# Computing the keys and values of a token tile in eight half-width groups instead of four full-width ones

## What is computed

```python
xn = _layernorm(x, axis=-1)
# attention branch
q = xn @ Wq + bq
kv = (xn @ Wdown + bdown) @ Wup + bup          # 1024 -> 256 -> 2048
q = q.reshape(B, T, H, Dh); kv = kv.reshape(B, T, H, 2 * Dh)
k, v = jnp.split(kv, 2, axis=-1)
q = apply_rope(q); k = apply_rope(k)
att = softmax(einsum('bthd,btgd->bthg', q, k) / sqrt(64))   # 16 x 16 per token
attn = einsum('bthg,btgd->bthd', att, v).reshape(B, T, D) @ Wout + bout
# expert branch: top-1 of 8
probs = softmax(xn @ router_w.T + router_b)
ffn = y_all[top1] * max(probs)
out = x + attn + ffn
```

## Time and profile before

| | us |
|---|---|
| median of 2 runs | 2858.91 |
| the 2 runs | 2851.67, 2866.16 |
| the profiled execution, on the device | 2871.62 |
| span of its slowest core (core 1) | 2870.1 |
| spans of its 8 cores | 2836.2 to 2870.1 |

### The profile page before, as it was taken

One profiled execution on the slowest core, in us unless ns is written; L12 is line 12 of the kernel. 1 busy time (PEld: TensorE's weight loads), 2 busy tenths in 40 slices (PEclk: granted clock), 3 DMA queues, 4 the chain that ended last, 5 costly groups with the idle time before them and its releaser, 6 DMA issues.

```text
span 2870.1 us, 38972 instructions; the slowest of 8 cores (2836.2 to 2870.1 us)
## 1 busy us (share of the span) xinstructions
PE 1937.4 (68%) x16622; PEld 1561.4 (54%) x16622; DVE 859.9 (30%) x1041; ACT 558.5 (19%) x770; POOL 106.6 (4%) x210
## 2 busy tenths in 40 slices
PE   0112268687776868686868778686868687777867
PEld 0112247465665746564756556564647475665646
DVE  2111132332324242323333232423232332324241
ACT  0122231221212030312122121203031211212030
POOL 0000000000000000000000000000000000000000
PEclk9956569688887869696978778787969787887869
DMA  5465515142332414151524234251415152332413
GB/s 161 138 206 199 190 59 206 59 178 87 141 124 91 175 59 174 38 201 59 192 73 177 88 118 147 80 185 39 169 58 206 59 184 81 140 125 94 157 59 132
DMA packets 60798, 366.45 MB, mean 128 GB/s; under 512 B 7107, under 2 KB 8131, under 8 KB 26580
## 3 DMA queue, kind: packets, MB, share of 16 engines
q1 hardware_dynamic: 31828, 179.41, 18.8%
q0 software_dynamic: 28800, 184.56, 16.9%
HBM read 330.39 MB, written 33.55 MB: 127 GB/s over the span
## 4 chain that ended last, share of the span: by engine, by line
PE 58%; DMA 17%; DVE 9%; ACT 8%; issue 4%; DVEq 2%; ACTq 2%; SPq 1%; POOL 0%; POOLq 0%
PE psb L814 26%; DMA exbuf<-exscratch 10%; PE psb L764 7%; PE psb L729 5%; DMA y_f<-exw 5%; PE psb L866 4%; PE psa L721 4%; ACT koct L584 2%; ACT vdm L589 2%; PE psa L752 2%; PE psa L879 2%; DVE exbuf L299 1%; ACTq L509 1%; DVEq L216 1%; DVE pav L463 1%
## 5 line engine op out<-in xcount | busy, mean ns | idle before, releaser
L814 PE MATMUL psb<-xe,exbuf 128*128 128x256 bf16 x8192 | 971.4, 284 | 131.5 <-DVE xe L472 68.8
L814 PEld LDWEIGHTS psb<-xe,exbuf 128*128 128x128 bf16 x8192 | 827.6, 102 | 278.3 <-issue 155.9
L764 PE MATMUL psb<-lat,wup_sb 128*128 128x256 bf16 x1024 | 187.8, 361 | 122.9 <-ACTq L509 122.9
L472 DVE TENSOR_TENSOR xe<-xnf,mrep 128x2048 bf16<-128x2048 bf16 x96 | 116.2, 1224 | 471.1 <-PE psb L814 467.3
L764 PEld LDWEIGHTS psb<-lat,wup_sb 128*128 128x128 bf16 x1024 | 123.8, 125 | 187.3 <-issue 149.5
L695 PE MATMUL psa<-idbf,exbuf 128*128 128x128 bf16 x512 | 47.5, 270 | 203.5 <-DVE exbuf L299 198.3
L721 PE MATMUL psa<-rT_sb,xnf 128*128 128x8 f32 x512 | 111.5, 361 | 89.7 <-DVEq L216 89.7
L721 PEld LDWEIGHTS psa<-rT_sb,xnf 128*128 128x128 f32 x512 | 110.4, 332 | 93.2 <-issue 93.2
L695 PEld LDWEIGHTS psa<-idbf,exbuf 128*128 128x128 bf16 x512 | 43.3, 125 | 207.6 <-issue 207.5
L729 PE MATMUL psb<-xnf,wq_sb 128*128 128x256 bf16 x1024 | 154.1, 328 | 0.0
L729 PEld LDWEIGHTS psb<-xnf,wq_sb 128*128 128x128 bf16 x1024 | 122.1, 120 | 30.9
(11 more groups left out here) (123 smaller groups left out, 1620.7 us busy)
## 6 DMA issues: line engine op xcount, KB each, us to landing
exbuf<-exscratch SPq DMA_DIRECT2D x128, 1024.0 KB, 5.5
exbuf<-exscratch POOLq DMA_DIRECT2D x128, 1024.0 KB, 8.5
y_f<-exw SPq DMA_DIRECT2D x64, 512.0 KB
x_t<-x POOLq DMA_DIRECT2D x32, 512.0 KB, 5.1
exscratch<-exbuf POOLq DMA_DIRECT2D x8, 2048.0 KB, 10.6
out<-outsb POOLq DMA_DIRECT2D x32, 512.0 KB, 6.8
y_f<-wq SPq DMA_DIRECT2D x8, 512.0 KB
y_f<-wo SPq DMA_DIRECT2D x8, 512.0 KB
```

Source lines behind the costliest of these rows:

```text
L472: vector.tensor_tensor(out=re(xe[:, 2048 * (ex_i % 2):2048 * (ex_i % 2) + 2048], "p (cc t) -> p cc t", t=256), in0=src0, in1=m1.broadcast_ ...
L764: li = tensor.matmul(out=psb[:, 256 * gch:256 * (gch + 1)], lhsT=wup[:, 4096 * k + 128 * ch: 4096 * k + 128 * (ch + 1)], rhs=lat[:, 256 * ...
L814: li = tensor.matmul(out=pout(m), lhsT=exbuf[:, eb + 1024 * k + 128 * m: eb + 1024 * k + 128 * (m + 1)], rhs=xe[:, xb + 256 * k:xb + 256 * ...
```

## The change

The up-projection is cut into eight groups `kv0` to `kv7` of 8 matmuls (4 chunks) each, which write the lower and the upper half of `psb` (two banks each) in turn. TensorE waits before group r for the eviction of group r-2 and no longer for that of group r-1; the first two groups wait for `latev` and `qev`. ScalarE evicts each half with an instruction of 1024 elements per partition, with runs of 4 elements in the target instead of 8. The waits of VectorE and of the later `psb` user move from `kv1ev` to `kv3ev` and from `kv3ev` to `kv7ev`, which mark the same data.

```diff
 T_SLOTS = ['xnT', 'router', 'q', 'prepA', 'prepB', 'lat', 'kv0', 'kv1', 'kv2', 'kv3',
+           'kv4', 'kv5', 'kv6', 'kv7',
            'vT0', 'qk0', 'vT1', 'qk1', 'av0', 'av1', 'expert', 'wout', 'yT']
 S_SLOTS = ['apply', 'den', 'qev', 'latev', 'kv0ev', 'kv1ev', 'kv2ev', 'kv3ev',
+           'kv4ev', 'kv5ev', 'kv6ev', 'kv7ev',
            'vst0', 'extr0', 'vst1', 'exp0', 'extr1', 'exp1', 'of0', 'of1', 'nrinv']
...
@@ VectorE
                 vector.wait_ge(smS, sv(i, 'qev'))
-                vector.wait_ge(smS, sv(i, 'kv1ev'))
+                vector.wait_ge(smS, sv(i, 'kv3ev'))
...
-                vector.wait_ge(smS, sv(i, 'kv3ev'))
+                vector.wait_ge(smS, sv(i, 'kv7ev'))
...
@@ ScalarE
-                for r in range(4):
+                for r in range(8):
                     scalar.wait_ge(smT, tv(i, 'kv%d' % r))
                     if r == 0 and i > 0:
                         scalar.wait_ge(smT, tv(i - 1, 'qk1'))
-                    if r == 2 and i > 0:
+                    if r == 4 and i > 0:
                         scalar.wait_ge(smT, tv(i - 1, 'vT1'))
-                    if r < 2:
-                        srck = re(psb[:], "p (g og j) -> p og j g", og=32, j=8)
+                    hb = 1024 * (r % 2)
+                    if r < 4:
+                        srck = re(psb[:, hb:hb + 1024], "p (g og j) -> p og j g",
+                                  og=32, j=8)
                         dstk = re(koct[:], "p (og j gg) -> p og j gg", j=8,
-                                  gg=16)[:, :, :, 8 * r:8 * r + 8]
+                                  gg=16)[:, :, :, 4 * r:4 * r + 4]
                         scalar.copy(out=dstk, in_=srck)
                     else:
...
@@ TensorE
-                for r in range(4):
-                    tensor.wait_ge(smS, sv(i, 'latev'))
-                    tensor.wait_ge(smS, sv(i, 'qev') if r == 0 else sv(i, 'kv%dev' % (r - 1)))
-                    for gch in range(8):
-                        ch = 8 * r + gch
+                for r in range(8):
+                    if r == 0:
+                        tensor.wait_ge(smS, sv(i, 'latev'))
+                        tensor.wait_ge(smS, sv(i, 'qev'))
+                    elif r >= 2:
+                        tensor.wait_ge(smS, sv(i, 'kv%dev' % (r - 2)))
+                    hb = 1024 * (r % 2)
+                    for gch in range(4):
+                        ch = 4 * r + gch
                         for k in range(2):
-                            li = tensor.matmul(out=psb[:, 256 * gch:256 * (gch + 1)],
+                            li = tensor.matmul(out=psb[:, hb + 256 * gch:
+                                                       hb + 256 * (gch + 1)],
...
-                tensor.wait_ge(smS, sv(i, 'kv3ev'))
+                tensor.wait_ge(smS, sv(i, 'kv7ev'))
```

More of the change, by code:

```diff
@@ L577, in _ @@
                         scalar.wait_ge(smT, tv(i - 1, 'qk1'))
-                    if r == 2 and i > 0:
+                    if r == 4 and i > 0:
                         scalar.wait_ge(smT, tv(i - 1, 'vT1'))
-                    if r < 2:
-                        srck = re(psb[:], "p (g og j) -> p og j g", og=32, j=8)
+                    hb = 1024 * (r % 2)
+                    if r < 4:
+                        srck = re(psb[:, hb:hb + 1024], "p (g og j) -> p og j g",
+                                  og=32, j=8)
                         dstk = re(koct[:], "p (og j gg) -> p og j gg", j=8,
-                                  gg=16)[:, :, :, 8 * r:8 * r + 8]
+                                  gg=16)[:, :, :, 4 * r:4 * r + 4]
                         scalar.copy(out=dstk, in_=srck)
                     else:
-                        srcv = re(psb[0:64, :], "p (g og j) -> p og j g", og=32, j=8)
+                        srcv = re(psb[0:64, hb:hb + 1024], "p (g og j) -> p og j g",
+                                  og=32, j=8)
                         dstv = re(vdm[:], "p (og j gg) -> p og j gg", j=8,
-                                  gg=16)[:, :, :, 8 * (r - 2):8 * (r - 2) + 8]
+                                  gg=16)[:, :, :, 4 * (r - 4):4 * (r - 4) + 4]
                         scalar.copy(out=dstv, in_=srcv)
```

## The result

| | before | changed |
|---|---|---|
| median, us (10 and 11 runs) | 2868.65 | 2735.95 |
| ratio, 95% interval | | 0.9513 [0.9484, 0.9542] |
| profiled execution, us | 2871.62 | 2736.39 |
| spans of the cores, us | 2836.2 to 2870.1 | 2703.4 to 2734.8 |

The changed kernel is 4.9% faster: 0.0487 x 2868.65 = 140 us, where 115 us were forecast.

A forecast was written before the change was run, and what follows sets the result against it. The bound was taken to be TensorE and ScalarE in strict turns in the up-projection. 20.4 - 13.2 = 7.2 us per tile, times 16 = 115 us; 2858.9 - 115 = 2744 us (-4.0%), range 2705 to 2795 us.

The forecast's parts named there:

- What bounds the stage: Up-projection: TensorE matmuls and ScalarE evictions take strict turns with nothing beside them, 20.4 us a tile.
- Evictions: ScalarE's half evictions of 1024 elements in the up-projection: 1.05 us each, pitch 1.20 us with drain and signal.
- C: Rival: up-projection evictions cost by the run, a half takes 1.865 us; gain 50 us, 2809 us; chance 0.05.
- E: Rival: slower, short runs make a half eviction cost 2.435 us; +24 us, 2883 us; chance 0.03.
- I take the third: Clock case chosen for the up-projection: four groups low, then high; last eviction ends at 13.1 us.
- the 20.4 us before: Length per tile of the up-projection stage before the change, first matmul to VectorE's addition to the values (L407).
- The level of VectorE and ScalarE: End of the up-projection: VectorE free after q and k at 13.1 us, the same moment as `kv7ev`.
- No gain behind the stage: From `vT0` on the order is unchanged and the chain only moves up; no gain counted there.
- A: Rival: low clock for the whole up-projection stage, 15.1 us per tile; gain 85 us, 2774 us; chance 0.20.
- B: Rival: high clock throughout the up-projection stage, 10.9 us per tile; gain 152 us, 2707 us; chance 0.10.
- the forecast: Main case: up-projection stage falls from 20.4 to 13.2 us per tile; gain 115 us, 2744 us; chance 0.57.
- D: Rival: gain given back in the expert phase, TensorE's 62.3 us weight waits doubling; 2806 us; chance 0.05.

The follow-up runs named there:

- e9: e1 with six extra unused matmuls behind each half group, so turns stay but the clock is high; ratio to the kernel before 1.0008, stage 20.86 us.
- e4: Kernel before the change with 10 extra unused matmuls behind each of the four groups, filling TensorE's pauses; ratio to before 0.9846, stage 18.94 us.
- e1: Changed kernel with eight half groups, but TensorE waits for the eviction of the group just before (r-1), so no overlap; ratio to before 1.0256.
- e7: Changed kernel with 8 extra unused matmuls in TensorE's pause between the latent's matmuls and the up-projection; ratio to before 0.9478, stage 12.27 us.
- e2: Changed kernel with VectorE's addition to q moved ahead of its wait for kv3ev; ratio to before 0.9513.
- e3: Changed kernel with four half buffers in psb and psa instead of two, TensorE waiting for the eviction of group r-4; ratio to before 0.9530.
- e5: Changed kernel with q addition moved forward and four half buffers, ScalarE evicting keys and VectorE values with their bias; ratio to before 0.9300, stage 10.04 us.

## Why the prediction was right

**What bounds the stage.** TensorE and ScalarE in turns, with nothing beside them: right. e9 against the changed kernel shows 7.66 us per tile for the overlap, at a clock that was slightly higher in e9.

**Evictions.** 1.05 us were taken, 1.012 and 1.005 were measured; 1.20 us of pitch were taken, 1.16 measured. Rivals C and E needed 1.87 and 2.44 us and are out. No cost of the short runs is to be seen: 1012 ns with runs of 4 is not above the 1053 ns of the contiguous copy, and 2 x 1012 is 159 ns above 1865, which one fixed part per instruction would explain. The estimate from the Trainium skill ("ScalarE: Activation LUTs", What ACT_TABLE_LOAD costs), 1.04 us, is 3% above the trace; the page's figures are for ACTIVATE, and the instructions here are CAST.

**The clock: the step that was mis-sized.** "I take the third" stood for four groups, 32 matmuls, at the low clock. The traces have 14 to 19 in three tiles of four and none in the fourth, 12.3 on the mean. The fault was a misreading of rows 2. There the prediction says that the clock rose during `kv1`, "some 7 us on". Three stretches of that tile, `kv0` and the beginning and the end of `kv1` (length; busy us and instructions of PE, PEld, DVE, ACT, POOL; granted clock; DMA share; GB/s) say otherwise:

```profile
1171.15:1174.60 3.45, 3.45 (x16) 2.23 (x16) 0.00 (x0) 0.00 (x0) 0.00 (x0) 0.50 0.00 0
1176.90:1178.00 1.10, 1.10 (x11) 0.98 (x12) 0.00 (x0) 0.00 (x0) 0.00 (x0) 1.00 0.00 0
1178.10:1179.40 1.30, 1.29 (x7) 0.60 (x4) 0.00 (x0) 0.00 (x0) 0.00 (x0) 0.50 0.00 0
```

`kv0` ran at the low clock, and `kv1` began at the high one. Its 2.51 us are not a rise but a fall: the clock went back during it, after the pause of 2.2 us ahead of it. So 16 low matmuls came before the rise, not 32. A group of mixed speed does not tell which way the clock went. It is the rule and not this tile: of the 91 tiles of the kernel before whose stage begins at the low clock, 82 have the first 16 matmuls low and the 17th high. So the changed kernel does not raise its clock any sooner; it holds on to it, since the pauses are short.

With two groups low instead of four the prediction's own prices give 1.68 + 1.89 + 0.14 = 3.7 us for the start of the second eviction, 3.7 + 7 x 1.20 = 12.1 us for the end of the last, and 12.2 us for L409. The pitch of 1.16 us takes off 0.3 more. The traces have 11.85 us in the 94 tiles that begin at the low clock, 10.6 in the 34 others, and 11.5 on the mean, not 13.2. That is 1.7 x 16 = 27 us too little gain. Against it stands an error the other way: the 20.4 us before were those of core 1, the slowest, and the mean of all cores is 19.8, 10 us less in all. 115 + 27 - 10 = 132 us is what the traces show, and the ratio of the runs makes it 140. That the two errors partly cancel is luck.

The level of VectorE and ScalarE was right: on the mean VectorE is done with k at 11.27 us and ScalarE at 11.36 us.

**No gain behind the stage.** Right: 14.49 against 14.68 us, and 70.17 against 70.29.

**Rivals.** A (low clock throughout) is out with 52 of 64 matmuls at the high clock. The rule named with it, in the Trainium skill ("TensorE: Matmul & The Clock Gate", A second HAM failure mode: psum-queue depth-cycling), has short idles between groups make the clock oscillate; here pauses of 0.18 to 0.45 us between groups left it high to the end of the stage, and in e4 even pauses of 1.0 us did. It was e1, with pauses of 1.3 us between bursts of 1.86 us, that had the low clock. B (high clock throughout) is what 34 of the 128 tiles did and what e7 makes of the stage. It had a chance of 0.10 beside 0.57 for the forecast, and the stage of 11.5 us came nearer to its 10.9 us than to the forecast's 13.2. In the time the two are about equally far off: gains of 152 and 115 us, where the ratio gives 140 and the traces 132. D is out: the stretch of the experts takes 70.17 us and took 70.29. The waits for their weights, 53.5 us after 62.3, prove nothing by themselves, as e2 shows; how far the eight cores' loads hinder one another was not tested.

## What to carry to other kernels

Where the chain of waits alternates between two engines, halve the unit and let them overlap; the floor is the slower engine's pitch, fixed part and drain included, so ask first who evicts and whether a second engine can share it, since more buffers and less work beside it brought nothing here (e2, e3). Splitting without overlap was worse than leaving it (e1). TensorE's pauses have a second price, the clock of the matmuls that follow, and it can be measured by itself by filling the pauses with matmuls of no use. When the clock rises and falls is to be read from the granted clock, stretch by stretch, and not guessed from a group whose matmuls were in part slow.

## What was not expected of the hardware

- Bursts of 8 matmuls (1.86 us) with pauses of 1.3 us ran at 1.2 GHz for 60 of 64 matmuls (e1), bursts of 16 with pauses of 2.2 us for 34 of 64 (before), and with six extra matmuls in each pause only some 11 of all 112 were low (e9). The kernel got 2.5 points faster by 768 matmuls per core more: 1.0256 to 1.0008.
- Eight extra matmuls in one pause of 1.2 us ahead of the stage took the low ones from 12.3 to 0.2 (e7).
- VectorE's read of 1024 f32 elements of PSUM with an addition took 1.22 us on 64 partitions (e5), 0.2 us more than ScalarE's plain eviction of the same size.
